# Latent attention: context from unsplit F32 rows in two 64-column halves of the array, row sums added apart, latent queries in column halves

## Chip, core and metric

One Trainium2 chip, one NeuronCore of it. The metric is the device time of one execution in microseconds; lower is better.

## What is computed

Two transformer layers on x (16 batches of 100 rows of 256) with a context of 16 x 1444 rows of 64. Each layer has a cross attention to the context and a mixture of experts. The change touches the attention of the first layer only:

```python
q_hk = (hidden_q @ Wq.T).reshape(Bv, Sv, H, K)            # H = 16 heads
q_big = jnp.einsum('bshk,hkq->bshq', q_hk, w_kc_q)
q_big = _apply_rope(q_big, ...)                           # 192 values a head
kv_r = _apply_rope(kv_c, ...)                             # 1444 keys of 64
q_r = jnp.einsum('bshq,hqr->bhsr', q_big, W_qr)
k_r = jnp.einsum('bld,hdr->bhlr', kv_r, W_kr)
attn = jax.nn.softmax(jnp.einsum('bhsr,bhlr->bhsl', q_r, k_r), axis=-1)
ctx_c = jnp.einsum('bhsl,bld->bhsd', attn, kv_r)
ctx_lat = jnp.einsum('bhsd,hkd->bhsk', ctx_c, w_kc_kv)
return ctx_lat.transpose(0, 2, 1, 3).reshape(Bv, Sv, H * K) @ Wo.T
```

The kernel folds the weights, so that queries and context rows meet in the 64 latent values: a score is a latent query (64) times a rotated context row (64), and the context is softmax weights times the same rotated rows.

## The kernel before

The stages run one behind the other; between them all engines meet. **fold_weights** (L205) makes the folded weights, among them M2, written twice side by side (L237) so that the 64 latent columns fill partitions 0-63 and 64-127.

**latent_queries** (L267) goes over 4 chunks of 400 columns (4 batches x 100 rows) and 16 heads. For each head TensorE makes two halves of 96 rows in split products (twelve F32R matmuls, L175), VectorE multiplies with the rope tables (L353), GpSimd adds (L375), TensorE narrows with M2 in plain F32 (L315), ScalarE rounds to F32R (L385), VectorE subtracts to get the low part in the lower 64 partitions (L344), and SyncE stores the head (L303).

**latent_attention** (L388) goes over 16 batches. A batch's 1600 query columns (16 heads x 100) are cut into 4 groups of 400, the keys into 12 tiles of 128, so a batch has 48 steps. Step n does, in the order in which each engine's program is written:

- TensorE: two score matmuls in F32R (L792 on 128 rows: high query parts and low query parts against the high key part; L793 on 66 rows: the low key part and two rows with the negative row maximum, high and low). For the next batch, one "max piece" (L578), 39 in all, scores without exponential in two banks. Then the values of step n-4: three F32R matmuls (L175 with EH, EL and KVH, KVL) that add high and low parts; the context rows have a column of ones, so that row 64 of the result is the row sum.
- ScalarE: the exponential (L742) to E, and one step later its rounded copy EH (L733).
- GpSimd: EL = E - EH (L501) for 43 of the 48 steps; VectorE does five.
- VectorE: the reduction of each max piece (L599), the rotation of the keys of the batch after next in parts (L527 to L549), the reciprocals of the row sums (L623), the division (L631), the addition to X (L618).

Once a batch the maxima are turned by TensorE (L583), split into MH and ML (L589, L593), and two small DMAs write them into QB (L488). Step 0 of the next batch waits for them. The row sums go by DMA to SR, the reciprocals by DRAM to RS, divided heads to CT, and the projection (L612, 8 F32 matmuls) adds them up. SyncE also loads the queries and the keys (L477) of later batches, in one order written out by hand.

The waits are counted semaphores. Two counts matter here: a max piece waits until the piece two before it is reduced (two banks, FB), and an exponential until the slot in E is free.

## Time and profile before

| | us |
|---|---|
| median of 3 runs | 2293.81 |
| lowest, highest | 2281.6, 2295.21 |
| the profiled execution | 2283.25 |
| its span, first to last instruction | 2281.4 |

| engine | busy us | share of the span |
|---|---|---|
| TensorE, matmuls | 1857.9 | 81% |
| TensorE, weight loads | 1632.6 | 72% |
| VectorE | 1492.1 | 65% |
| ScalarE | 1220.5 | 53% |
| GpSimd | 1117.1 | 49% |

Weight loads run beside matmuls. A matmul's duration has the time that it takes through the array in it, which the next one overlaps, so distances between starts tell what the stream costs. The mean granted TensorE clock is 0.905 of full speed over the span.

### The profile page before, as it was taken

The numbers are of one execution on the slowest core, as the hardware profiler recorded it, in microseconds if no ns is written. First come the engines' busy times: TensorE is split into PE (matmuls) and PEld (weight loads), VectorE is DVE, ScalarE is ACT, GpSimd is POOL, SyncE is SP. The second block draws the span as 40 slices with busy tenths as digits, with TensorE's granted clock in tenths as the row PEclk, the third lists the DMA queues.
The fourth block names the chain that finished last, engine by engine and source line by source line (L and its number), as shares of the span: only waits on it lengthen the run. The fifth ranks groups of instructions, "written<-read, shape, count | busy, mean of one in ns | idle before, by whom it ended". The sixth has DMA issues, their size and how long they took to land. (4 is left out here: it accounts for less than half of the span.)

```text
span 2281.4 us, 38538 instructions
## 1 busy us (share of the span) xinstructions
PE 1857.9 (81%) x10550; PEld 1632.6 (72%) x10550; DVE 1492.1 (65%) x2799; ACT 1220.5 (53%) x2996; POOL 1117.1 (49%) x961
## 2 busy tenths in 40 slices
PE   4999958999999999999999973499993689837870
PEld 3677736888888888888888963499993466626870
DVE  4677777777777777767776433377774466656763
ACT  2111115777777767767777851366661266515650
POOL 0455528888788888878888852300004100014005
PEclk9999967999999999999999985699996599958985
DMA  5522251111111111111110002455542100026654
GB/s 159 197 58 57 55 176 55 63 63 63 45 54 63 64 31 63 63 64 63 63 54 11 16 8 78 140 197 196 204 165 58 34 1 0 0 77 196 198 164 113
DMA packets 115748, 195.76 MB, mean 86 GB/s; under 512 B 48213, under 2 KB 94265, under 8 KB 110161
## 3 DMA queue, kind: packets, MB, share of 16 engines
q1 hardware_dynamic: 107409, 180.88, 24.6%
q0 software_dynamic: 8192, 13.15, 2.0%
q8 instruction: 65, 1.06, 0.2%
q14 instruction: 82, 0.67, 0.1%
HBM read 147.01 MB, written 46.63 MB: 85 GB/s over the span
## 5 line engine op out<-in xcount | busy, mean ns | idle before, releaser
L501 POOL TENSOR_TENSOR EL<-E,EH 128x400 fp32r<-128x400 f32 x688 | 833.4, 1239 | 158.5 <-ACT EH L733 154.0
L599 DVE TENSOR_REDUCE PM<-bank 128x1 f32<-128x482 f32 (+1 forms) x624 | 397.2, 650 | 185.9 <-PE bank L578 182.9
L742 ACT ACTIVATE E<-bank 128x400 f32<-128x400 f32 x768 | 386.4, 503 | 212.8 <-PE bank L793 153.2
L733 ACT ACTIVATE EH<-E 128x400 fp32r<-128x400 f32 x768 | 407.0, 532 | 0.0
L175 PE MATMUL bank<-EH,KVH 128*128 128x400 f32 x768 | 283.1, 369 | 19.8 <-POOL EL L501 18.5
L578 PE MATMUL bank<-KH,QS 128*128 128x482 f32 (+1 forms) x624 | 250.9, 414 | 53.9 <-DVE KVL L549 27.6
L1248 POOL DMA_INDIRECT m_back<-rows_out,m_slots x64 | 64.8, 1013 | 450.8 <-DMA rows_out<-m_ys 421.2
L792 PE MATMUL bank<-QS,KH 128*128 128x400 f32 x768 | 272.1, 354 | 14.9 <-issue 9.1
L793 PE MATMUL bank<-QB,KB 66*128 66x400 f32 x768 | 269.1, 350 | 0.0
L175 PE MATMUL bank<-EH,KVL 128*128 128x400 f32 x768 | 265.7, 346 | 0.0
L175 PE MATMUL bank<-EL,KVH 128*128 128x400 f32 x768 | 265.5, 346 | 0.0
L1232 POOL DMA_INDIRECT rows_in<-m_XN,m_slots x64 | 66.2, 1034 | 340.9 <-POOLq L951 265.6
L375 POOL TENSOR_TENSOR rotated<-rope_prod 96x400 f32<-96x400 f32 x128 | 131.9, 1051 | 169.7 <-DVE rope_prod L353 169.2
L175 PEld LDWEIGHTS bank<-EH,KVH 128*128 128x128 f32 x768 | 146.6, 191 | 64.9 <-POOL EL L501 53.4
L175 PE MATMUL bank<-m_xh,m_UH 128*116 128x256 f32 (+1 forms) x620 | 183.2, 296 | 2.1 <-DVE m_xl L1380 1.4
L175 PE MATMUL bank<-m_xh,m_UL 128*116 128x256 f32 (+1 forms) x620 | 178.0, 287 | 0.0
L175 PE MATMUL bank<-m_xl,m_UH 128*116 128x256 f32 (+1 forms) x620 | 177.8, 287 | 0.0
L578 PEld LDWEIGHTS bank<-KH,QS 128*128 128x128 f32 x624 | 123.6, 198 | 74.5 <-DVE PM L599 43.9
L353 DVE TENSOR_TENSOR rope_prod<-bank,rope_q 96x400 f32<-96x400 f32 x256 | 128.9, 563 | 51.3 <-PE bank L175 51.1
L792 PEld LDWEIGHTS bank<-QS,KH 128*128 128x128 f32 x768 | 146.2, 190 | 20.8 <-issue 10.7
L175 PEld LDWEIGHTS bank<-EL,KVH 128*128 128x128 f32 x768 | 146.2, 190 | 14.5
L793 PEld LDWEIGHTS bank<-QB,KB 66*128 66x128 f32 x768 | 146.2, 190 | 0.6
(244 smaller groups left out, 3983.3 us busy)
## 6 DMA issues: line engine op xcount, KB each, us to landing
m_stage_u<-in_m_up SPq DMA_DIRECT2D x20, 1392.0 KB
raw<-in_ctx_T SPq DMA_DIRECT2D x16, 1444.0 KB, 6.1
m_xg<-rows_in SPq DMA_DIRECT2D x55, 256.0 KB, 4.1
rows_out<-m_ys SPq DMA_DIRECT2D x55, 256.0 KB, 3.7
m_stage_d<-in_m_down SPq DMA_DIRECT2D x20, 696.0 KB
queries<-q_out SPq DMA_DIRECT2D x64, 200.0 KB, 2.4
QS<-queries SPq DMA_DIRECT2D x16, 800.0 KB, 6.1
rows_in<-zeros SPq DMA_DIRECT2D x5, 1792.0 KB
```

The lines of the kernel that those rows point to most:

```text
L175: ins = nc.tensor.matmul(out, lhs, rhs, start=first and n == 0, stop=last and n == len(todo) - 1)
L353: last = nc.vector.tensor_tensor(prod[:, h % 2, n, :].rearrange("p (b s) -> p b s", b=CB), psum[2 * (h % 2) + half][0:HALF, 0:CH].rearrang ...
L375: last = nc.gpsimd.tensor_tensor(rot[:, h % TURNS, half, :], prod[:, h % 2, 2 * half, :], prod[:, h % 2, 2 * half + 1, :], ALU.add)
L501: ops.tensor_tensor(EL[:, n % PB, :], E[:, n % EB, :], as_f32(EH[:, n % PB, :]), ALU.subtract).then_inc(sem, 1)
L578: nc.tensor.matmul(psum[F0 + f % banks][:, 0:KW[j]], QS[r][:, t * P:(t + 1) * P], KH[r][:, sum(KW[:j]):sum(KW[:j + 1])], start=True, stop= ...
L599: nc.vector.tensor_reduce(PM[:, f:f + 1], psum[F0 + f % f_banks(b)][:, 0:KW[f % KC]], AX.X, ALU.max).then_inc(red_done, 1)
L733: nc.scalar.activation(EH[:, n % PB, :], E[:, n % EB, :], ACT.Copy).then_inc(hi_done, 1)
L742: nc.scalar.activation(E[:, n % EB, :], psum[S0 + n % SB][:, 0:CH], ACT.Exp).then_inc(exp_done, 1)
L792: nc.tensor.matmul(out, KH[r][:, keys], QS[r][:, cols], start=True, stop=False)
L793: nc.tensor.matmul(out, KB[r][:, keys], QB[r][:, cols], start=False, stop=True).then_inc(s_ready, 1)
L1232: pool.indirect_dma_start(rows_in[:, :], bass.IndirectOffsetOnAxis(slots[:, n, b:b + 1], 0), XN[:, b, :], None).then_inc(scattered, 16)
L1248: pool.indirect_dma_start(back[:, b % RING, n, :], None, rows_out[0:tiles * TOK, :], bass.IndirectOffsetOnAxis(slots[:, n, b:b + 1], 0)).t ...
```

## The change

**Values.** The exponentials are no longer split into EH and EL, and the context rows no longer into KVH and KVL. One step now covers 800 query columns: of a half batch (p) of 8 heads, the even heads (o = 0) and the odd heads (o = 1), 400 columns each, in two neighbouring banks. One exponential instruction covers both. Two F32 matmuls of 64 output columns each bring the context of the even heads to partitions 0-63 and that of the odd heads to 64-127 of one bank. A batch has 24 steps; TensorE does them in pairs m, with the values of the pair before behind the scores.

**Row sums.** The column of ones is gone. VectorE adds the exponentials of the even heads, four steps at a time (tensor_reduce over a strided view, in two parts of 200 columns), GpSimd those of the odd heads, step by step. A matmul with ones adds up the partitions, for each half batch.

**Order.** Two max pieces a step (EP = 2), still two banks. Ten of twelve parts of the key rotation move from VectorE to GpSimd; the two that make the low key part stay, at steps 18 and 20. The turn of the maxima is in pair 10 of 12, ScalarE's and VectorE's part of it at step 22. The key loads of the batch after go out when the low key part is complete (step 20), the two maxima DMAs behind them.

**Set-up.** KB and QB have 128 rows (maxima in rows 1 and 2, a padding row 0), with more to fill before the first batch; the queries load only after that.

**Latent queries** are narrowed in pairs of heads: the even head to partitions 0-63, the odd one to 64-127, high and low parts in two tiles, four stores a pair. M2 is written once.

```diff
-                    nc.tensor.matmul(psum[2 + h % 2][0:HALF, half * P:(half + 1) * P],
-                                     wqr[:, h, half * HALF:(half + 1) * HALF],
-                                     wkr[:, h, :].rearrange("p (o d) -> p o d", o=1).to_broadcast([R0, 2, DC]),
-                                     start=True, stop=True)
+                    nc.tensor.matmul(psum[2 + h % 2][0:HALF, half * DC:(half + 1) * DC],
+                                     wqr[:, h, half * HALF:(half + 1) * HALF], wkr[:, h, :], start=True, stop=True)
...
+                    for row, part in enumerate((out_h, out_l)):
+                        for o in range(2):
+                            sp.dma_start(queries[bass.ts(c, CB)].rearrange("b p h s -> p h b s")[row * DC:(row + 1) * DC, 2 * j + o],
...
                     for half in range(2):
-                        last = nc.tensor.matmul(psum[4 + h % 2][:, 0:CH], M2[:, half, h, :], rot[:, h % TURNS, half, :],
-                                                start=half == 0, stop=half == 1)
+                        for o in range(2):
+                            h = 2 * j + o
+                            last = nc.tensor.matmul(psum[4 + j % 2][o * DC:(o + 1) * DC, 0:CH], M2[:, half, h, :],
+                                                    rot[:, h % TURNS, half, :], start=half == 0, stop=half == 1)
...
-                        if h >= 2:
-                            narrow(c, h - 2)
+                        if h >= 3 and h % 2:
+                            narrow(c, h // 2 - 1)
...
-    SB, FB = 3, 2
-    EB, PB = 4, 6
-    BEHIND = 4
+    SB, FB = 2, 2
+    GT = 4
+    EB = 2 * GT
+    EP = 2
...
-    TURN_AT, HI_AT = 42, 26
-    RECIP_AT, CT_AT, OUT_AT = 9, 17, 20
-    ROT_AT = (3, 5, 7, 10, 11, 12, 13, 19, 21, 24, 32, 34, 37)
-    LOW_ON_VECTOR = (39, 41, 43, 45, 47)
+    SUM_AT, SUM0_AT, OUT_AT, TURN_AT = 2, 7, 8, 10
+    RECIP_AT, CT_AT = 9, 14
+    ROT_AT = (3, 4, 5, 6, 8, 9, 10, 11, 13, 14)
+    HI_AT, LO_AT = (17, 18), (18, 20)
...
+        def sum_even(v, b, g, part):
+            cols = slice(part * (CH // 2), (part + 1) * (CH // 2))
+            p, q = divmod(g, KT // GT)
...
+                src = R[:, base:base + 1 + GT, 0, cols]
...
+            nc.vector.tensor_reduce(out, src.rearrange("p t c -> p c t"), AX.X, ALU.add).then_inc(even_sum, 1)
+
+        def sum_odd(pool, b, n):
...
+            nc.gpsimd.tensor_tensor(out, first, R[:, slot(n), 1, :], ALU.add).then_inc(odd_sum, 1)
+
+        def sums(pe, b, p):
...
+            for o in range(2):
+                last = nc.tensor.matmul(psum[MISC][o * DC:(o + 1) * DC, 0:CH], ones[:], ES[:, p, o, :], start=True, stop=True)
...
+                def scores(b, n):
...
+                    for lhs, rhs in ((KH, QS), (KB, QB)):
+                        heads = rhs[r][:, p * 2 * CH:(p + 1) * 2 * CH].rearrange("p (j o s) -> p o j s", o=2, s=S)
+                        for o in range(2):
+                            last = nc.tensor.matmul(psum[S0 + 2 * (n % SB) + o][:, 0:CH].rearrange("p (j s) -> p j s", s=S),
+                                                    lhs[r][:, keys], heads[:, o], start=lhs is KH, stop=lhs is KB)
...
-                    split_products(nc, psum[A0 + g % 2][:, 0:CH],
-                                   [(KVH[b_mod(b)][:, cols], KVL[b_mod(b)][:, cols], EH[:, n % PB, :], EL[:, n % PB, :])],
-                                   first=t == 0, last=t == KT - 1).then_inc(av_done, 1)
+                    for o in range(2):
+                        last = nc.tensor.matmul(psum[CTX][o * DC:(o + 1) * DC, 0:CH], KV[b_mod(b)][:, t, :], R[:, slot(n), o, :],
+                                                start=t == 0, stop=t == KT - 1)
+                    last.then_inc(av_done, 1)
...
+                    for m in range(NS // 2):
+                        for n in (2 * m, 2 * m + 1):
+                            scores(b, n)
...
+                            for f in range(EP * n, min(EP * n + EP, NF)):
+                                if has_next:
+                                    max_piece(pe, b + 1, f)
...
+                        for n in (2 * m - 2, 2 * m - 1):
+                            if n >= 0:
+                                values(b, n)
...
                 def step(b, has_next, has_keys):
                     for n in range(NS):
...
+                        pieces = [f for f in range(EP * n, min(EP * n + EP, NF)) if has_next]
+                        for f in pieces:
+                            reduce_piece(v, b + 1, f)
+                        if n % GT < 2:
+                            if n >= GT:
+                                sum_even(v, b, n // GT - 1, n % GT)
```

## Rows read from the trace of the kernel before

**Rows 1.** Windows: PE, PEld, DVE, ACT, POOL busy us (x count), clock, DMA share, GB/s
```profile
100.00:330.00 230.00, 201.32 (x900) 150.62 (x898) 168.33 (x321) 32.00 (x62) 117.42 (x114) 0.95 0.28 82
...
357.00:1375.00 1018.00, 942.80 (x4696) 852.66 (x4696) 705.71 (x959) 750.02 (x1660) 837.30 (x691) 0.98 0.16 51
```

**Rows 2.** Tile ML, window 400:1300: ns min/median/max, first to last start us
```profile
L488 SPq DMA_DIRECT2D QB<-ML x15: 759/804/1093, 417.7 to 1294.9; - x15
```

**Rows 3.** Timeline of attention steps: start us, us, engine, line
```profile
705.14 0.35 PE L792 MATMUL bank<-QS,KH 128*128 128x400 f32 x1
...
705.51 0.38 PE L578 MATMUL bank<-KH,QS 128*128 128x482 f32 x1
...
705.73 0.34 PE L175 MATMUL bank<-EH,KVH 128*128 128x400 f32 x1
...
705.95 0.65 DVE L599 TENSOR_REDUCE PM<-bank 128x1 f32<-128x482 f32 x1
...
711.95 0.34 PE L792 MATMUL bank<-QS,KH 128*128 128x400 f32 x1
```

**Rows 4.** Timeline: the projection's F32 passes, merged
```profile
699.63 3.40 PE L612 MATMUL bank<-BB,CT 128*100 128x256 f32 x15
```

**Rows 5.** Lines by shape, TensorE: busy us, mean ns of one, idle before
```profile
L315 PE MATMUL bank<-rotated,M 96*128 96x400 f32 x256 | 96.2, 500 | 2.2 <-POOL rotated L375 2.2
...
L612 PE MATMUL bank<-BB,CT 128*100 128x256 f32 x256 | 62.4, 400 | 14.0 <-DVE CT L631 14.0
```

**Rows 6.** Waits, window 357:1375: us in total, times, longest us
```profile
PEld bank L175 <- POOL EL L501: 53.4, 136, 1.0
PEld bank L578 <- DVE PM L599: 34.2, 30, 3.8
...
PE bank L792 <- DMA QB<-ML: 5.7, 6, 3.6
```

**Rows 7.** Timeline of the latent queries: one head's narrowing, merged
```profile
90.54 1.51 PE L315 MATMUL bank<-rotated,M 96*128 96x400 f32 x4
```

**Rows 8.** Timeline of the weight folding: one head (in brackets: idle before)
```profile
56.37 0.65 PE L241 MATMUL bank<-wo,wkv 128*64 128x256 f32 x2
56.95 0.46 PEld L237 LDWEIGHTS bank<-wkr,wqr 64*96 64x96 f32 x4 [0.39 <-issue]
...
57.55 0.65 PE L241 MATMUL bank<-wo,wkv 128*64 128x256 f32 x2
```

**Rows 9.** Lines by shape, GpSimd
```profile
L501 POOL TENSOR_TENSOR EL<-E,EH 128x400 fp32r<-128x400 f32 x688 | 833.4, 1239 | 158.5 <-ACT EH L733 154.0
...
L527 POOL TENSOR_TENSOR raw<-raw,ropeT 128x722 f32<-128x722 f32 x4 | 6.7, 1717 | 37.4 <-DMA rawk<-in_ctx_k 37.4
```

**Rows 10.** Lines by shape, VectorE
```profile
L599 DVE TENSOR_REDUCE PM<-bank 128x1 f32<-128x482 f32 x416 | 268.1, 650 | 101.0 <-PE bank L578 99.7
...
L527 DVE TENSOR_TENSOR raw<-raw,ropeT 128x722 f32<-128x722 f32 x60 | 71.4, 1194 | 3.9 <-DMA rawk<-in_ctx_k 3.9
...
L631 DVE TENSOR_TENSOR CT<-CU,RS 64x800 f32<-64x800 f32 x32 | 56.1, 1752 | 11.2 <-DMA RS<-recips 10.9
...
L623 DVE RECIPROCAL RR<-SR 16x100 f32<-16x100 f32 x16 | 12.1, 755 | 7.1 <-DMA SR<-CU 7.1
```

**Rows 11.** Tile raw, window 400:1300: one operation, and the key loads' way to landing
```profile
L538 DVE TENSOR_TENSOR raw<-raw x26: 898/900/902, 447.5 to 1211.0; 128x722 f32<-128x722 f32 x26
...
DMA to landing us min/median/max: 5.8/6.1/6.3
```

**Rows 12.** Timeline of the attention's start: memsets, first maxima, first scores
```profile
310.36 1.26 DVE L824 MEMSET KB<- 2x1444 f32 x1 [0.34 <-issue]
...
320.39 0.34 DVE L829 CAST KVH<-there 128x24 fp32r<-128x24 f32 x3 [1.20 <-DMA there<-in_key_ones]
...
355.13 0.28 DVE L593 TENSOR_TENSOR ML<-bank,MH 13x128 fp32r<-13x128 f32 x1 [0.78 <-ACT MH L589]
...
358.44 0.70 PE L792 MATMUL bank<-QS,KH 128*128 128x400 f32 x1 [3.64 <-DMA QB<-ML]
```

**Rows 13.** Line L303: the latent queries' stores
```profile
L303 SPq DMA_DIRECT2D queries<-q_out x64: 371/372/4186, 83.0 to 304.9; - x64
```

More of the change, by code:

```diff
@@ L52, in __init__ @@
         self.nc, self.ctx = nc, ctx
-        self.psum = [ctx.enter_context(nc.psum_tensor(f"bank{i}", [P, PSUM_COLS], F32)) for i in range(8)]
+        self.banks = ctx.enter_context(nc.psum_tensor("banks", [P, 8, PSUM_COLS], F32))
+        self.psum = [self.banks[:, i, :] for i in range(8)]
         self.stats = fixed(ctx, nc, "stats", [S, B, 6])
@@ L467, in latent_attention @@
         cu_done = core.sem("at_cu")
+        sum_done = core.sem("at_sum")
+        su_done = core.sem("at_su")
         sr_in = core.sem("at_sr")
@@ new lines, in sum_odd @@
+        def sum_odd(pool, b, n):
+            p, t = divmod(n, KT)
+            if t == 0:
+                return
+            pool.wait_ge(exp_done, b_val(b) * NS + (n + 1 + SB))
+            done = b_val(b) * 2 * ADDS + (p * ADDS + t - 1)
+            if t > 1 or p or b is not FIRST:
+                pool.wait_ge(odd_sum, done)
+            if t == KT - 1 and b is not FIRST:
+                pool.wait_ge(sum_done, b_val(b) * 2 + (p - 1))
+            first = R[:, slot(n - 1), 1, :] if t == 1 else EA[:]
+            out = ES[:, p, 1, :] if t == KT - 1 else EA[:]
+            nc.gpsimd.tensor_tensor(out, first, R[:, slot(n), 1, :], ALU.add).then_inc(odd_sum, 1)
@@ L749, in step @@
[L749 to L756 removed]
+                            act.wait_ge(odd_sum, odd_sums_to(before(b), NS + n - EB))
@@ new lines, in step @@
+                        k = S0 + 2 * (n % SB)
+                        nc.scalar.activation(R[:, slot(n), :, :], banks[:, k:k + 2, 0:CH], ACT.Exp).then_inc(exp_done, 1)
+                        if n in HI_AT and has_keys:
+                            keys_high(act, b + 2, HI_AT.index(n))
+                        if n == 1 and b is not FIRST:
+                            context_out(act, before(b), 1)
+                        if n == 2 * SUM_AT + 1 and b is not FIRST:
+                            sums_out(act, before(b), 1)
@@ L808, in step @@
                             turn_max(pe, b + 1)
-                steps(pe, step)
-                for n in range(NS - BEHIND, NS):
-                    values(Batch(0, B - 1), n)
-                project(pe, Batch(0, B - 1))
+                        for n in (2 * m - 2, 2 * m - 1):
+                            if n >= 0:
+                                values(b, n)
+                            elif b is not FIRST:
+                                values(before(b), NS + n)
+                        if m == SUM_AT and b is not FIRST:
+                            sums(pe, before(b), 1)
+                        if m == SUM0_AT:
+                            sums(pe, b, 0)
+                        if m == OUT_AT and b is not FIRST:
+                            pe.wait_ge(su_done, b_val(b) * 2 + 1)
+                            project(pe, before(b))
+                steps(pe, step)
+                for n in range(NS - 2, NS):
+                    values(LAST, n)
+                pe.wait_ge(res_done, B - 1)
+                sums(pe, LAST, 1)
+                pe.wait_ge(su_done, 2 * B)
+                project(pe, LAST)
             @block.vector
```

376 lines of the change are left out of this document (186 added, 190 removed).

## Prediction, made before the changed kernel was run

> **What bounds the kernel now.** I read the engine totals of the page first: TensorE leads. Busy time of matmuls overlaps, so the stages come next: the attention stage takes 1018 us of 2281, TensorE busy 943 of it, and the latent queries before it 230 us [rows 1]. The instruction that loads the low half of the row maxima runs once a batch; its first and last start give (1294.9-417.7)/14 = 62.66 us a batch [rows 2].
>
> What TensorE does in one batch follows from starts, not durations. Six steps with a max piece in each last 711.95-705.14 = 6.81 us, 1.135 a step; the piece of 482 columns takes the stream 0.22 of it, which leaves 0.183 for each of the five F32R matmuls of 400 columns [rows 3]; I count 0.182. The output projection's F32 matmuls count two passes each, the last lasting 0.40, so (3.40-0.40)/14 = 0.215 us a pass [rows 4, 5]. A batch has 48 score steps of 2 matmuls and 48 value steps of 3, so 240 x 0.182 = 43.7 us; 39 max pieces, 8.6; 16 projection passes, 3.4; the turn of the maxima, 0.3. That is 56.0 of 62.66; 6.6 us a batch are waits. The list of waits names them: TensorE waits, most often with the weight load of a matmul, for the low parts EL and for the maxima's reductions, and seldom for the maxima's DMAs [rows 6]. So the stage is bound by TensorE, closely followed by GpSimd (837 us).
>
> **Values.** Before: 144 F32R matmuls a batch, 26.2 us. After: 24 steps of two F32 matmuls of 64 output columns, one into partitions 0-63, one into 64-127. The F32 matmul of 400 columns exists in the latent queries: four passes in 1.51 us, the last lasting 0.50, so (1.51-0.50)/3 = 0.337 us a pass, two passes a matmul [rows 5, 7]. Whether two halves of the array work at once no row shows. One bound: one after the other, 96 x 0.337 = 32.4 us. Other bound: side by side. If matmuls start in order, the two steps of a run (A1 A2 B1 B2 A3 A4 B3 B4, where A and B are the halves) take five slots and not eight, since B1 can go with A2, B2 with A3, B3 with A4, but B4 is alone: 5 x 0.337 = 1.69 us, 12 runs a batch, 20.2 us. I take side by side, because the two write separate partitions and read separate weights, and nothing in the trace makes the second wait. The Trainium skill (TensorE: Matmul & The Clock Gate, Packing small matmuls) says that column tiles start about 4 ns apart and run together; no row here shows it, and its ideal of four slots would make 16.2 us of the 20.2.
>
> **Changes of shape.** In the weight folding, passes on 64 rows alternate with passes that fill 64 columns. From one L241 to the next is 57.55-56.37 = 1.18 us; six passes hold 4x128 + 2x256 columns, 0.86 us at 0.84 ns (0.337/400); between them weight loads stand still for 0.39 us with nothing to wait for [rows 8]. That leaves 0.32 us for two changes, 0.16 each. The context changes to halves and back once per pair of steps: 24 x 0.165 = 4.0 us a batch. The two row-sum pairs follow directly on a context run, three slots each: 2.0 us. The Trainium skill (TensorEngine Tiling (Array Packing), Key Properties) states that changing the tiling mode drains the array; the idle 0.39 us agrees.
>
> TensorE after: scores 96 x 0.182 = 17.5 (same columns; the low product is on 128 rows now and not 66, and L793 with 66 starts at the same pace as the others), values 20.2, changes 4.0, sums 2.0, max pieces 8.6, projection 3.4, turn 0.3: 56.0 us. The old sum again. TensorE gains nothing; what moves are the waits.
>
> **Waits that go.** ScalarE loses 48 rounding copies, VectorE and GpSimd the 48 subtractions that make EL. GpSimd gets 22 additions (1.24 us each) and the rotation's 6,636 columns, at 1717/722 = 2.4 ns: 27 + 16 = 43 us [rows 9], under a batch. The cover: rows of eight steps may wait for it. Its ninth rotation part, for which ScalarE's key copy at step 17 waits, comes at about 10 us (three steps at 2.6, the exponential) + 10 x 1.24 + 5,868 x 0.0024 = 36.5 us; step 17 comes at 44 us. Were that cover gone, exponentials would queue behind the key copy. So the EL waits end.
>
> The context has one bank now, and each half batch's first value matmul waits for its copy on ScalarE; 1.46 us of scores and up to 0.9 of max pieces stand in between, so it costs nothing. The projection's new wait for the row sums' copy has an iteration of cover as well; behind it would stand all scores. SyncE issues two DMAs for one at the divisors and four for two at the queries, 0.4 us each [rows 13], off the path.
>
> **Waits that come: the reductions.** Now four max pieces come in one iteration of two steps, with two banks, and between them VectorE also adds the even rows. Counting from the first piece: a reduction starts 0.44 us after its piece and lasts 0.65 [rows 3, 10]. Pieces at 0 and 0.22; reductions end at 1.09 and 1.74; the third piece, with its load, can start at 1.34 and the fourth at 1.99, where 1.39 to 1.61 was due. From there to the next first piece 0.22 + 0.165 + 1.69 + 0.165 + 0.73 = 2.97. In iterations with a quarter sum, its two parts (800 to 1000 elements, 933 in the mean) stand ahead of reductions. No row has such a strided reduction. Bounds: 1.12 us, as VectorE runs undisturbed (L538's 900 ns for 722 elements less L599's 650 for 482 make 1.04 ns an element, plus 0.15), and 2.0 us, near the 1752/800 ns of the disturbed L631 [rows 10, 11]. I take 1.3, nearer the plain read, since it has one source. Then two iterations last 10.17 us where 8.74 would do: 1.4 lost, five times, 6.8 us a batch (the last iteration has a piece less). At 1.12 it is 6.0, at 2.0 13.8. The reciprocal (0.755 us) sits in the same queue: 0.8 more. The other VectorE work (division, now one instruction of 128x800; two rotation parts) falls where a bank isn't due.
>
> **Waits that come: the maxima's way round.** In the first batch it took 358.44-355.13 = 3.3 us from the low subtraction to the score matmul [rows 12]. Behind the turn TensorE still has 5.5 us of work; ahead of the subtraction VectorE has two sum parts and a rotation part (3.8 us), which just fits. But SyncE issues the next key loads right before, at the twentieth step of 24, and these take 6.1 us to land [rows 11]; if the small DMAs come behind them, the next batch starts about 2.3 us late. Bounds 0 and 3, I take 1.0.
>
> A batch: 56.0 + 6.8 + 0.8 + 1.0 = 64.6 us, +1.95; 16 batches +31 us.
>
> **Latent queries and the ends.** A head costs 12 x 0.182 + 4 x 0.337 = 3.53 us, and the 63 intervals between the first and last query store, (304.9-83.0)/63, make 3.52 us [rows 7, 13]: pure TensorE. After: per pair of heads 8 passes in five slots and two changes, 1.69 + 0.33 against 2.70, so 32 x 0.68 = -22 us. Weight folding computes half the columns of M2: 16 x 4 x 64 x 0.84 ns = -3. Memsets: 1.26 us for 1,444 columns; 8,248 columns a buffer instead of 3,400 make +12.6 us, less the 1.2 us of waiting for a constant that they cover [rows 12] and the KVL part: +10, on the path since queries load only behind them. The last batch's extra matmul and DMAs: +2. Together -13.
>
> 2283.25 (the profiled execution's time, 0.5% under the median of 2293.81) + 31 - 13 = **2301 us**. Measured medians may stand some 10 above. Between 1% under and over the median of before lie 2271 to 2317; that 1% is about what a measurement of this kernel can tell from no change.
>
> **Rivals.**
> *A, the halves overlap fully and changes are free, faster.* Four slots, no 0.165: 56.0 - 4.0 - 14 x 0.337 = 47.3 us. But the reductions' queue stays: after the fourth piece now 2.30 in place of 2.97 us, two iterations last 9.5 us where 7.4 would do, 10.1 us a batch; with the reciprocal's 0.8 and 1.7 for the maxima (less work behind the turn) 59.9 us, -44. Latent queries 32 x 1.35 = -43, ends +9: 2205 us. For it: nothing shows the tail slot. Against it: the standstill in [rows 8]. It decides from about 1.2 us a batch below the forecast on.
> *B, no concurrency, slower.* 32.4 + 2.7 + 29.8 + 4.0 = 68.9, waits 6.5 (the longer runs cover more): 75.4 us, +204; latent queries 32 x 0.33 = +11, ends +9. 2507 us. For it: all F32 rows here are serial. Against it: separate partitions and weights.
> *C, strided sums hold the reductions, slower.* Parts of 2.0 us: 13.8 in place of 6.8, +7 us a batch: 2413 us. At 1.6 us a part it is 10: 2352 us. For it: VectorE's SBUF rows swell beside GpSimd (1194 ns in the mean for 722 columns, [rows 10], against 900). Against it: one source only. The Trainium skill (Vector Engine (DVE) Microarchitecture Reference, Measured stream behaviour on trn2) gives 1.73 ns in place of 1.05 when a source hops every element; an estimate from it is 1.6 us a part. No row here shows such a read.
>
> **Chances.** Forecast (2250 to 2335) 0.45, A 0.22, C 0.18, B 0.15. Of the forecast's 0.45 I put 0.07 under 2271, 0.29 between and 0.09 above 2317. Faster: 0.22 + 0.07 = 0.29. Same: 0.29. Slower: 0.18 + 0.15 + 0.09 = 0.42. The likeliest case's own range is 2250 to 2335; for 8 in 10 the range reaches to A at 2200 and C at 2415 and leaves B out.
>
> **What would show it.** Right: value passes of the two halves whose passes start in pairs 0.34 us apart; a batch of 64 to 65 us; third and fourth pieces waiting for reductions in every iteration; no wait for GpSimd; 3.2 us a head. Wrong: a run of four F32 matmuls over 2.5 us (B), sum parts over 1.6 us (C), context runs of 1.35 us with no gap beside them (A), exponentials waiting for odd sums.

## The result and the profile after

| | before | after |
|---|---|---|
| median, us | 2294.51 (4 runs) | 2380.68 (4 runs) |
| lowest to highest | 2281.6 to 2297.24 | 2379.42 to 2381.73 |
| span of the profiled execution | 2281.4 | 2379.9 |
| mean granted TensorE clock | 0.905 | 0.869 |

After over before is 1.0387, with a 95% interval of 1.0347 to 1.0427: slower by some 86 us. The forecast was 2301, its range 2200 to 2415.

Engine totals of the changed kernel, then its line for the TensorE clock in 40 slices of the span:

```profile
PE 1824.5 (77%) x9910; PEld 1307.4 (55%) x9910; DVE 1531.4 (64%) x2720; ACT 824.3 (35%) x1796; POOL 869.7 (37%) x762
...
PEclk9999859989989989998998997599997599957995
```

ScalarE lost 396 us of work and GpSimd 247, as the change intends, and TensorE's matmuls are busy for 33 us less. None of it shortened the kernel. Before, the attention's slices stood at 0.98 of the full clock [rows 1]; now many stand at 8 and 9 tenths.

The tile of the low maxima, as in [rows 2]:

```profile
L493 SPq DMA_DIRECT2D QB<-ML x16: 752/809/820, 348.7 to 1391.3; - x16
...
  PE banks L816: 79.1, 15
  PEld banks L816: 14.7, 4
```

The last two lines say what waited for this tile: TensorE's matmuls (PE) and its weight loads (PEld), us in total and how often. From first to last start it is (1391.3-348.7)/15 = 69.5 us a batch, where it was 62.6. The attention lost 15 x 6.9 = 104 us. Its first maxima come at 348.7 instead of 356.4, so what lies ahead gained 8. TensorE's matmuls stood 79.1 us for this tile, 5.3 a batch.

The two lines must not be added. A weight load and the matmul behind it can both be listed for one and the same standstill: at 1260.16 us the load has 6.67 us of idle time before it and the matmul 5.97, for the same maxima. In what follows a standstill is the matmul's row; the row of the weight load alone may lie beside a matmul that still runs.

The changed kernel's waits, window 400 to 1400 us (14.4 batches), in total, times, longest:

```profile
PEld banks L562 <- DVE PM L583: 122.3, 199, 2.2
...
ACT CU L646 <- DVE CT L657: 87.8, 14, 6.4
PE banks L816 <- DMA QB<-ML: 75.4, 14, 6.1
...
PE banks L562 <- DVE PM L583: 54.4, 40, 1.9
...
PEld banks L827 <- ACT CU L646: 15.4, 12, 1.3
...
PE banks L827 <- ACT CU L646: 14.0, 14, 1.1
```

The wait for GpSimd's low parts [rows 6] is gone, and three others stand there. A max piece waits for reductions: the matmuls stand 54.4/14.4 = 3.8 us a batch, and the weight loads' 122.3/14.4 = 8.5 lies partly beside running matmuls. The next batch's first score waits for the maxima's DMA. And one value run in each batch waits for the context's copy, 14.0/14 = 1.0 us, because ScalarE waits with it for VectorE's division (the 12 waits of the weight loads are at the same places as 12 of the 14 of the matmuls).

VectorE's sums of the even rows, grouped by shape (L610; a third form, into ES, has 1928 ns):

```profile
L610 DVE TENSOR_REDUCE R<-R 128x200 f32<-128x1000 f32 x64 | 124.9, 1955 | 6.2 <-ACT R L781 5.7
...
L610 DVE TENSOR_REDUCE R<-R 128x200 f32<-128x800 f32 x64 | 101.6, 1589 | 4.8 <-ACT R L781 4.7
```

A part takes 1.59 to 1.96 us, where the forecast had 1.3.

**The values.** A run of eight context passes in the timeline of the changed kernel (start us, us, engine, line):

```profile
705.21 1.56 PE L827 MATMUL banks<-R,KV 128*64 128x400 f32 x8
705.60 0.14 PEld L827 LDWEIGHTS banks<-R,KV 128*64 128x64 f32 x2 [0.19 <-issue]
705.93 0.14 PEld L827 LDWEIGHTS banks<-R,KV 128*64 128x64 f32 x2 [0.19 <-issue]
706.70 0.63 PE L816 MATMUL banks<-QS,KH 128*128 128x400 f32 x2
```

Weights are loaded in pairs, one for each half of the array, 0.33 us apart. From the first pass to the score behind the run 706.70-705.21 = 1.49 us go by: four slots of 0.337 and one change of shape of 0.14 to 0.16. So the halves run side by side, and there is no fifth slot. The Trainium skill (TensorE: Matmul & The Clock Gate, Packing small matmuls) has column tiles run together; the trace agrees, with 1.49 us for eight passes that take 2.70 one after the other.

**The end of a batch.** The turn of the maxima and the next batch's start, same kernel and columns:

```profile
471.08 1.95 DVE L610 TENSOR_REDUCE R<-R 128x200 f32<-128x1000 f32 x1
...
473.06 0.91 DVE L541 TENSOR_TENSOR KB<-raw,KH 64x722 fp32r<-64x722 f32 x1
...
474.00 2.00 DVE L610 TENSOR_REDUCE R<-R 128x200 f32<-128x1000 f32 x1
...
474.15 0.34 SPq L482 DMA_DIRECT2D raw<-in_ctx_T  x1
...
474.68 0.33 SPq L483 DMA_DIRECT2D rawk<-in_ctx_k  x1
...
475.89 0.27 DVE L577 TENSOR_TENSOR ML<-banks,MH 13x128 fp32r<-13x128 f32 x1
476.18 0.88 SPq L493 DMA_DIRECT2D QB<-MH  x1
...
477.12 0.81 SPq L493 DMA_DIRECT2D QB<-ML  x1
...
482.07 1.03 PE L816 MATMUL banks<-QS,KH 128*128 128x400 f32 x2 [5.78 <-DMA QB<-ML]
```

The key loads go out at 474.15 and 474.68, while the subtraction still stands behind VectorE's last sum part; the two small DMAs stand behind them, and the score waits until 482.07, 4.95 us from the issue of the second. In the first batch before, with nothing ahead, it took 3.3 us from the low subtraction to the score [rows 12]; here 482.07-475.89 = 6.2.

**The clock.** Stretches of the same kernel, columns as in [rows 1] (the clock is the third number from the end):

```profile
482.00:488.00 6.00, 5.93 (x18) 4.42 (x20) 3.80 (x5) 1.68 (x2) 0.98 (x1) 0.51 0.00 0
511.00:515.00 4.00, 3.35 (x10) 1.30 (x10) 2.41 (x5) 0.00 (x0) 4.00 (x3) 0.59 0.21 47
525.00:529.00 4.00, 3.56 (x12) 1.24 (x12) 0.92 (x2) 1.84 (x3) 2.73 (x2) 0.57 0.01 4
700.00:705.00 5.00, 4.11 (x20) 2.42 (x16) 4.99 (x7) 2.40 (x4) 2.52 (x3) 1.00 0.00 0
...
500.00:1200.00 700.00, 588.48 (x2522) 348.72 (x2520) 479.67 (x573) 228.44 (x307) 384.86 (x316) 0.91 0.16 51
```

Three times in the batch that begins at 482.07 the granted clock falls to the lower level (1.2 of 2.4 GHz): with the standstill of 5.78 us for the maxima, after 1.83 us for a reduction at 511.65, and after 1.18 and 1.00 us for a reduction and the context's copy at 523.38 and 525.44. There a run of eight context passes lasts 2.94 us instead of 1.56. Over 700 us the mean is 0.91. With two levels, 1 and 0.5, this is 18% of the time at the lower one, 12.5 us of a batch. It costs up to half of that, 6.3 us; what of it falls into a standstill costs nothing more. Before, the same stretch had 0.99.

**What the batch loses, term by term.** The starts of the matmuls in the trace allow a finer count. Each distance from one matmul's start to the next is set against the distance that the same pair of instructions keeps at full clock when nothing waits (the shortest tenth). The excess belongs to the wait that ended there, or, where the lower level was granted and nothing waited, to the clock. For the changed kernel, over 15 batches, this gives 7.6 us a batch for reductions (the 3.8 above is only the part in which no matmul is recorded; a matmul's duration covers a short standstill behind it), 4.8 for the maxima, 1.1 for the context's copy and 4.8 for the clock. What is left of 69.5 is 51.3 us of work at full clock; the same count on the kernel before leaves 56.

### The profile page after: what moved, and what is told of

The parts are those of the page before. It is cut to its first block and busy times, and to the rows that moved or that the text cites. A ratio compares the mean times of both kernels' runs of the same rounds, so it can differ in the third digit from the quotient of the medians.

```text
span 2379.9 us, 34375 instructions
## 1 busy us (share of the span) xinstructions
PE 1824.5 (77%) x9910; PEld 1307.4 (55%) x9910; DVE 1531.4 (64%) x2720; ACT 824.3 (35%) x1796; POOL 869.7 (37%) x762
## 5 line engine op out<-in xcount | busy, mean ns | idle before, releaser
L583 DVE TENSOR_REDUCE PM<-banks 128x1 f32<-128x482 f32 (+1 forms) x624 | 379.3, 651 | 317.3 <-PE banks L562 316.5
L781 ACT ACTIVATE R<-banks 128x800 f32<-128x800 f32 x384 | 315.6, 839 | 545.5 <-PE banks L816 527.6
L625 POOL TENSOR_TENSOR EA<-EA,R 128x400 f32<-128x400 f32 x288 | 312.3, 1084 | 299.9 <-ACT R L781 293.1
L562 PE MATMUL banks<-KH,QS 128*128 128x482 f32 (+1 forms) x624 | 255.8, 465 | 111.7 <-DVE PM L583 58.3
L827 PE MATMUL banks<-R,KV 128*64 128x400 f32 x1536 | 326.5, 549 | 14.9 <-ACT CU L646 14.9
L816 PE MATMUL banks<-QS,KH 128*128 128x400 f32 x768 | 238.9, 394 | 79.2 <-DMA QB<-ML 79.1
L610 DVE TENSOR_REDUCE R<-R 128x200 f32<-128x1000 f32 (+1 forms) x128 | 226.4, 1772 | 10.9 <-ACT R L781 10.5
L816 PE MATMUL banks<-QB,KB 128*128 128x400 f32 x768 | 211.4, 358 | 0.0
L176 PE MATMUL banks<-m_xh,m_UH 128*116 128x256 f32 (+1 forms) x620 | 184.1, 297 | 11.4 <-issue 10.0
L176 PE MATMUL banks<-m_xh,m_UL 128*116 128x256 f32 (+1 forms) x620 | 178.6, 288 | 0.0
L610 DVE TENSOR_REDUCE ES<-R 128x200 f32<-128x1000 f32 x64 | 123.1, 1928 | 6.6 <-ACT R L781 6.6
```

The lines of the kernel that those rows point to most:

```text
L176: ins = nc.tensor.matmul(out, lhs, rhs, start=first and n == 0, stop=last and n == len(todo) - 1)
L562: nc.tensor.matmul(psum[F0 + f % n][:, 0:KW[j]], QS[r][:, t * P:(t + 1) * P], KH[r][:, sum(KW[:j]):sum(KW[:j + 1])], start=True, stop=True ...
L583: nc.vector.tensor_reduce(PM[:, f:f + 1], psum[F0 + f % f_banks(b)][:, 0:KW[f % KC]], AX.X, ALU.max).then_inc(red_done, 1)
L610: nc.vector.tensor_reduce(out, src.rearrange("p t c -> p c t"), AX.X, ALU.add).then_inc(even_sum, 1)
L625: nc.gpsimd.tensor_tensor(out, first, R[:, slot(n), 1, :], ALU.add).then_inc(odd_sum, 1)
L781: nc.scalar.activation(R[:, slot(n), :, :], banks[:, k:k + 2, 0:CH], ACT.Exp).then_inc(exp_done, 1)
```

## The experiments

Period is the time of one batch of the attention (first to last start of the maxima's low DMA, over 15). The clock is the mean granted over 500 to 1200 us of the profile. Ratios are against the kernel before on the same chip.

| | median us | ratio (95%) | period us | clock |
|---|---|---|---|---|
| before | 2278 to 2295 | 1 | 62.6 | 0.99 |
| after | 2380.68 | 1.0387 (1.0347 to 1.0427) | 69.5 | 0.91 |
| 1 latent queries alone | 2253.77 | 0.9886 (0.9837 to 0.9936) | 62.6 | 0.99 |
| 2 sums in memory order | 2256.23 | 0.9898 (0.9864 to 0.9932) | 62.8 | 0.95 |
| 3 maxima first | 2330.32 | 1.0233 (1.019 to 1.0277) | 67.3 | 0.92 |
| 4 one half of the array | 2449.03 | 1.0745 (1.07 to 1.079) | 74.0 | 1.00 |
| 5 low part early | 2356.9 | 1.0326 (1.0282 to 1.037) | 69.2 | 0.92 |
| 6 pieces apart | 2350.42 | 1.0247 (1.0216 to 1.0277) | 67.4 | 0.91 |
| 7 sums as additions | 2336.31 | 1.0175 (1.0142 to 1.0208) | 67.0 | 0.93 |
| 8 = 3 + 5 | 2298.14 | 1.002 (1.0001 to 1.004) | 64.2 | 0.96 |
| 9 = 3 + 5 + 7, division early | 2273.67 | 0.9916 (0.9893 to 0.994) | 62.6 | 0.96 |
| 10 = 3 + 5 + 2 | 2182.75 | 0.9567 (0.9523 to 0.961) | 57.5 | 1.00 |
| 11 = 3 + 5, division early | 2254.7 | 0.9885 (0.9837 to 0.9934) | 62.1 | 0.99 |
| 12 = 11 + 6 | 2182.55 | 0.9556 (0.9511 to 0.9601) | 57.6 | 1.00 |

The loss of each, counted as above from the starts of the matmuls, in us a batch (an estimate; each term may be off by some tenths):

| | reductions | maxima | copy | clock | left of the period |
|---|---|---|---|---|---|
| after | 7.6 | 4.8 | 1.1 | 4.8 | 51.3 |
| 2 sums in memory order | 3.3 | 4.5 | 1.1 | 2.5 | 51.4 |
| 3 maxima first | 7.5 | 2.7 | 1.1 | 4.7 | 51.5 |
| 4 one half of the array | 3.9 | 1.4 | 1.1 | 0.3 | 67.3 |
| 5 low part early | 7.2 | 4.8 | 1.1 | 4.7 | 51.4 |
| 6 pieces apart | 4.0 | 5.6 | 2.9 | 4.6 | 50.4 |
| 7 sums as additions | 6.5 | 4.6 | 0.9 | 3.8 | 51.3 |
| 8 = 3 + 5 | 8.2 | 1.1 | 1.0 | 2.4 | 51.6 |
| 9 = 3 + 5 + 7, division early | 7.7 | 1.0 | 0 | 2.5 | 51.5 |
| 10 = 3 + 5 + 2 | 3.6 | 1.0 | 1.1 | 0.3 | 51.6 |
| 11 = 3 + 5, division early | 8.5 | 1.2 | 0 | 0.7 | 51.8 |
| 12 = 11 + 6 | 3.9 | 1.9 | 0 | 0.2 | 51.6 |

The theory in them: two waits, for the reductions behind the strided sums and for the maxima's DMAs behind the key loads, make up the loss. The rivals: TensorE's own amount has grown (fifth slots, no concurrency), or GpSimd has become the bound.

**1, the latent queries alone.** The kernel before with fold_weights and latent_queries of the changed one (M2 of 64 columns a head, narrowing in pairs into two halves, four stores a pair).

> The kernel before with only the latent queries (and M2) in column halves; the attention is the old one. Theory (halves run pass beside pass in four slots, two changes of shape at 0.16 us a pair): a pair of heads 6.03 us instead of 7.05, 32 pairs, -33 us, so about 2261 against 2294. Rival (the four stores a pair in place of two, or the later low part, hold the queue): no gain or less than 10 us. Rival (five slots, as predicted): -22 us.

The first maxima's DMA started at 335.6 us instead of 356.4, and the period stayed at (1274.2-335.6)/15 = 62.6. So this part gains 21 us up to there, ratio 0.9886, and the loss of 104 us is the attention's. The number alone would have spoken for the rival with five slots (-22); the distances decide for four. The timeline of the changed kernel has the price of a change of shape: from the last of one head's F32R matmuls to the second behind the narrowing,

```profile
86.96 0.34 PE L176 MATMUL banks<-XH_a,AL 128*96 x1
...
87.23 1.56 PE L321 MATMUL banks<-rotated,M 96*64 96x400 f32 x8
...
88.99 0.34 PE L176 MATMUL banks<-XL_a,AH 128*96 x1
```

88.99-86.96 = 2.03 = 2 x 0.18 + 4 x 0.337 + 0.32: four slots and two changes of 0.16. Per pair it saves 2.70 - 1.35 - 0.32 = 1.03 us, 33 in all; with the folding's 3 that would be 36. At the borders of the four chunks the narrowing now waits 8.2 us in all for GpSimd, and the clock falls there, which it did not before. The stage before and in experiment 1, columns as in [rows 1]:

```profile
83.00:305.00 222.00, 218.32 (x976) 163.55 (x974) 159.19 (x307) 31.78 (x63) 126.08 (x123) 1.00 0.28 83
```

```profile
83.00:284.00 201.00, 189.11 (x965) 131.75 (x963) 134.33 (x272) 15.63 (x31) 124.13 (x121) 0.95 0.36 87
```

A clock of 0.95 over 201 us costs up to 10 us. Waits and clock together, up to 18, cover the 15 that are missing.

**2, the sums in memory order.** The same elements are read, but in the order in which they lie, so each output adds neighbours:

```diff
-            nc.vector.tensor_reduce(out, src.rearrange("p t c -> p c t"), AX.X, ALU.add).then_inc(even_sum, 1)
+            k = GT if q == 0 else GT + 1
+            nc.vector.tensor_reduce(out.rearrange("p (t c) -> p t c", t=k), src.rearrange("p t (c k) -> p t c k", k=k),
+                                    AX.X, ALU.add).then_inc(even_sum, 1)
```

> The changed kernel, with the even heads' sums read in the order of memory: the same elements, the same number of outputs, but each output adds neighbours (so the row sums are not the true ones). Theory (the stride makes a part 1.59 to 1.95 us, and this holds the reductions): a part falls to about 1.1 us, the reductions' waits fall by about 7 us a batch and the maxima's subtraction comes earlier, together 8 to 9 us a batch, 2380 to about 2245. Rival (the stride costs nothing, the number of elements does): parts stay above 1.5 us and the time within 10 us of 2380. Rival (batches are held by the maxima's way alone): parts fall, the time by less than 50 us.

```profile
L611 DVE TENSOR_REDUCE R<-R 128x200 f32<-128x1000 f32 x64 | 75.8, 1189 | 7.4 <-ACT R L783 7.0
...
L611 DVE TENSOR_REDUCE R<-R 128x200 f32<-128x800 f32 x64 | 62.4, 977 | 7.1 <-ACT R L783 7.1
```

The stride alone made the difference: for each element (1955-1589)/200 = 1.8 ns against (1189-977)/200 = 1.06. GpSimd, which works beside it, does not matter to the strided read: of the changed kernel's reductions of 128x1000, 5 have no GpSimd instruction beside them and take 1.83 to 1.97 us, and 17 have one throughout and take 1.92 to 1.98. The loss to reductions fell from 7.6 to 3.3 us a batch and that to the clock from 4.8 to 2.5; the maxima hardly moved (4.8 to 4.5), which I had expected to come earlier too. The period fell by 6.8 us where 8 to 9 were expected, the median by about 5%. The Trainium skill (Vector Engine (DVE) Microarchitecture Reference, Measured stream behaviour on trn2) has, for an operation of two sources, 1.73 ns where one of them hops every element and 1.05 where none does; the runs, with one source, agree within 0.1.

**3, the maxima first.** SyncE issues the maxima's two DMAs ahead of the key loads.

```diff
                     if has_keys:
-                        sp.wait_ge(k_ready, b_val(b) + 3)
-                        ...
-                            key_loads(sp, b_val(b + 3))
-                    if has_next:
-                        max_rows(sp, b_val(b + 1), b_mod(b + 1))
+                    if has_next:
+                        max_rows(sp, b_val(b + 1), b_mod(b + 1))
+                    if has_keys:
+                        sp.wait_ge(k_ready, b_val(b) + 3)
+                        ...
+                            key_loads(sp, b_val(b + 3))
```

> The changed kernel, with the two maxima DMAs ahead of the next key loads in SyncE's program. Theory (the small DMAs stand behind 1.8 MB of keys): the wait at a batch's start falls from 6 to about 3 us (what VectorE's late subtraction leaves), and the clock is cut less: -45 to -75 us, so 2305 to 2335. Rival (VectorE's queue alone makes them late): no change, 2375 to 2385. Rival (the key loads, now later, hold the next rotation): slower than 2381.

Its timeline at the same place as above:

```profile
473.89 0.27 DVE L577 TENSOR_TENSOR ML<-banks,MH 13x128 fp32r<-13x128 f32 x1
474.18 0.89 SPq L493 DMA_DIRECT2D QB<-MH  x1
...
475.12 0.81 SPq L493 DMA_DIRECT2D QB<-ML  x1
476.20 0.34 SPq L482 DMA_DIRECT2D raw<-in_ctx_T  x1
...
477.24 0.64 PE L817 MATMUL banks<-QS,KH 128*128 128x400 f32 x2 [2.97 <-DMA QB<-ML]
```

From the subtraction to the score 477.24-473.89 = 3.35 us, as in [rows 12]; behind the key loads it was 6.2. The loss to the maxima fell from 4.8 to 2.7 us a batch; the rest of it is a subtraction that comes late behind a sum part of 2 us. Period -2.2 us. By its ratio the run gained 35 us, less than the 45 to 75 expected, since the clock rose only from 0.91 to 0.92.

**5, the low part early.** VectorE subtracts at step 21, ahead of a sum part, and the DMAs stay behind the key loads.

```diff
+                        if n == 2 * TURN_AT + 1 and has_next:
+                            max_low(v, b + 1)
                         if n % GT < 2:
...
-                        if n == 2 * TURN_AT + 2 and has_next:
-                            max_low(v, b + 1)
```

> The changed kernel, with only VectorE's low subtraction ahead of the sum part of step 21; the key loads stay ahead of the maxima's DMAs. Theory (the small DMAs land with the key loads, whatever VectorE does, as long as they are issued behind them): the key loads go out at the same time as before, so the wait at a batch's start falls by less than 0.7 us a batch, 2365 to 2381. Rival (the two delays simply add): -2.0 us a batch and less of the clock's cut, 2330 to 2345.

The loss to the maxima stayed at 4.8 us a batch and the period came to 69.2, 0.3 less. With the key loads ahead, the place in VectorE's queue is worth next to nothing.

**8, both (3 and 5).**

> The changed kernel with two changes of order: the maxima's DMAs ahead of the key loads (as in the run before), and VectorE's low subtraction ahead of the sum part of step 21. Theory (the two queues add up: 2.9 us by the key loads, 2.0 by VectorE's sum part): the wait at a batch's start falls from 6 over 3.4 to about 1.4 us, 2380 - 50 - 30 = 2300. Rival (behind the subtraction something else is late, the turn itself or ScalarE): as with the DMAs alone, 2325 to 2345.

The loss to the maxima fell from 4.8 to 1.1 us a batch and that to the clock from 4.8 to 2.4, while reductions took 0.6 more; the period fell to 64.2, 5.3 us less. The edits are worth 2.2 and 0.3 one by one and 5.3 together: two queues in a row, of which the slower one hides the other.

**4, one half of the array.** Both value matmuls go into partitions 0 to 63, and the odd heads' own context is left out.

```diff
-                        last = nc.tensor.matmul(psum[CTX][o * DC:(o + 1) * DC, 0:CH], KV[b_mod(b)][:, t, :], R[:, slot(n), o, :],
-                                                start=t == 0, stop=t == KT - 1)
+                        last = nc.tensor.matmul(psum[CTX][0:DC, 0:CH], KV[b_mod(b)][:, t, :], R[:, slot(n), o, :],
+                                                start=t == 0 and o == 0, stop=t == KT - 1 and o == 1)
```

> The changed kernel, with both value matmuls of a step into partitions 0 to 63 (the even and odd heads' contexts are added up there, which leaves the odd heads' own context out). Theory (two halves run at once): eight passes take eight slots again, 2.7 us a run instead of 1.35, 12 runs, 16 us a batch, less what the longer run covers of other waits: 2380 to 2550 to 2640. Rival (the halves never overlap): within 10 us of 2381.

```profile
706.59 2.90 PE L827 MATMUL banks<-R,KV 128*64 128x400 f32 x8
...
706.98 0.14 PEld L827 LDWEIGHTS banks<-R,KV 128*64 128x64 f32 x1 [0.20 <-issue]
```

Now the loads come singly (the next of this kind at 707.32, 0.34 us later), and the eight passes take 2.90 us instead of 1.56: serial passes. That is rival B's machine, and it shows by contrast that the changed kernel's halves are concurrent. It adds 12 x 1.34 = 16.1 us of TensorE to a batch, but the period grew by 4.5 only, far less than expected: the reductions took 3.9 us in place of 7.6, the maxima 1.4 in place of 4.8, and the clock 0.3 in place of 4.8, at a granted 1.00. An engine that loses 18 us a batch to waits and the clock can be given 16 us of work for 4.5.

**6, the pieces apart.** The second step's two max pieces go behind the value run, so that no four come in a row.

```diff
-                            for f in range(EP * n, min(EP * n + EP, NF)):
-                                if has_next:
-                                    max_piece(pe, b + 1, f)
+                            if n % 2 == 0:
+                                for f in range(EP * n, min(EP * n + EP, NF)):
+                                    if has_next:
+                                        max_piece(pe, b + 1, f)
...
+                        for f in range(EP * (2 * m + 1), min(EP * (2 * m + 1) + EP, NF)):
+                            if has_next:
+                                max_piece(pe, b + 1, f)
```

> The changed kernel, with the third and fourth max piece of an iteration behind the value matmuls and not ahead of them; VectorE's program stays. Theory (four pieces within 1.6 us meet two banks, so TensorE stands until reductions are done): the waits for reductions, 12.6 us a batch in the changed kernel, fall by a third or more, 3 to 5 us a batch, 2380 to 2300 to 2330. Rival (VectorE simply has 8 x 0.65 + 2 x 1.85 = 8.9 us of work in two iterations, where TensorE has 8.0, and the order doesn't matter): less than 1 us a batch, 2365 to 2385.

The period fell by 2.1 us. Its waits, window 400 to 1400:

```profile
PE banks L816 <- DMA QB<-ML: 87.8, 15, 6.8
...
PEld banks L562 <- DVE PM L583: 81.0, 194, 1.1
...
PE banks L827 <- ACT CU L646: 46.2, 15, 3.3
PEld banks L827 <- ACT CU L646: 42.6, 12, 3.6
```

The reductions took 4.0 us a batch in place of 7.6. But the context's copy took 2.9 in place of 1.1 and the maxima 5.6 in place of 4.8: -3.6 + 1.8 + 0.8 = -1.0, and -0.2 for the clock; the remaining 0.9 lies in the column that is left. More than half of the gain was given back at the next waits in line, the division ahead of the copy above all.

**7, the sums as additions.** The four-step sum becomes additions of contiguous blocks of 128x800 (two steps each), a last one folds the two halves: no stride, and the sums remain complete.

```diff
-                src = R[:, base:base + 1 + GT, 0, cols]
...
+            pair = [R[:, base + 2 * k:base + 2 * k + 2, 0, :] for k in range(2)]
...
+                    nc.vector.tensor_tensor(AC[:], AC[:], pair[0], ALU.add).then_inc(even_sum, 1)
...
+                nc.vector.tensor_tensor(AC[:], AC[:], pair[1], ALU.add).then_inc(folded if last else even_sum, 1)
```

> The changed kernel, with the even heads' sums made by contiguous additions of 128x800 (two a quarter, one more of 400 at the end) in place of the strided reductions; the result is the true one. Theory (the stride is the cost, not the number of elements): a 128x800 addition takes 1.0 to 1.2 us where a part took 1.59 to 1.95, 5 to 6 us of VectorE instead of 11 for a half batch; the gain is that of the run that read in the order of memory, -100 to -130 us, 2250 to 2280. Rival (two-source reads beside GpSimd's additions swell to 1.7 us and more, on both engines): 2330 or slower.

```profile
L630 POOL TENSOR_TENSOR EA<-EA,R 128x400 f32<-128x400 f32 x288 | 346.7, 1204 | 265.5 <-ACT R L786 257.5
...
L610 DVE TENSOR_TENSOR AC<-AC,R 128x800 f32<-128x800 f32 x64 | 109.7, 1714 | 0.6
...
L606 DVE TENSOR_TENSOR AC<-AC,R 128x800 f32<-128x800 f32 x64 | 79.4, 1240 | 16.5 <-ACT R L786 16.5
```

Period -2.5 us, a third of what experiment 2 gave. One shape has means from 1240 to 1714 ns, and GpSimd's additions of 128x400 went from 1.08 to 1.20 in the mean. The timeline of the same run shows when an addition is slow:

```profile
618.82 0.98 DVE L606 TENSOR_TENSOR AC<-AC,R 128x800 f32<-128x800 f32 x1
620.17 1.03 POOL L630 TENSOR_TENSOR EA<-R 128x400 f32<-128x400 f32 x1 [9.59 <-ACT R L786]
...
647.00 1.75 POOL L535 TENSOR_TENSOR raw<-raw 128x722 f32<-128x722 f32 x1
647.52 2.08 DVE L606 TENSOR_TENSOR AC<-AC,R 128x800 f32<-128x800 f32 x1
```

Of the 160 additions of 128x800, 16 have no GpSimd instruction beside them: all take 0.98 us. Of the 44 that have one throughout, 39 take over 1.6. So the two engines hold each other up when VectorE adds from two sources in SBUF. No run took GpSimd's part away, but the contrast within this one leaves little else.

**9, order, additions and an earlier division** (`RECIP_AT, CT_AT = 7, 12` in place of 9, 14).

> The changed kernel with all: maxima's DMAs first, low subtraction first, contiguous additions, reciprocals at step 7 and division at step 12 in place of 9 and 14. Theory (three separate causes that add up: sums 6.8 us a batch, the maxima's way 6, its cut of the clock and the context's copy some 2): 69.5 - 14 = 55 to 58 us a batch, 2165 to 2215 us, which is under the kernel before. Rival (they hide one another; the reductions' bank wait takes what the others give): 2230 to 2260, equal to the additions alone.

The expectation had 55 to 58 us a batch, its rival 2230 to 2260 us, and the result is slower than both. The period is 62.6 us, that of the kernel before, and the gain of the median (0.8%) is about that of the latent queries: with the order right and no stride, but with the slow additions, the new attention is worth the old one.

**10, order and sums in memory order (2, 3 and 5).**

> The changed kernel with both changes of order and the even heads' sums read in the order of memory (row sums not the true ones). Theory (strided sums and the maxima's way are separate causes): their gains add, -6.8 and -5.2 us a batch, 69.5 to 57.5, about 2380 - 111 - 82 = 2187. Rival (both end in the same wait, the earlier reductions only move it to the maxima): 2215 to 2250.

Experiment 2 took about 111 us from the changed kernel, 8 about 84, each by its ratio; together 195, and here it is 188 (0.0820 of 2290). The two causes add up, and without them the change is 4.3% faster than before instead of 3.9% slower.

**11, order and the earlier division, strided sums kept.**

> The changed kernel with both changes of order, reciprocals at step 7 and division at step 12 in place of 9 and 14; sums strided. Theory (the context has one bank, and its copy waits for the division, TensorE 2 us a batch for the copy): -1 to -2 us a batch against the run with the order alone (2298), 2265 to 2285. Rival (the division only takes the place of another VectorE job in the same queue): 2290 to 2300.

Against 8 the period fell by 2.1 us. The value run's wait for the copy, 1.0 us a batch in 8, is gone, and the clock takes 0.7 in place of 2.4.

**12, order, earlier division, pieces apart.** It computes what the changed kernel computes and keeps the strided sums.

> A version meant to be fast, with the true result: the changed kernel with both changes of order, the third and fourth max piece behind the values, reciprocals at step 7 and division at step 12. Theory (each takes its own wait): order 82, pieces 30, division some 15 to 25 us: 2380 to 2245 to 2255, level with the old attention behind the new latent queries (2254 beside a before of 2278). Rival (VectorE's strided sums bound the first twenty steps at 8.9 us in two iterations, nothing more is to be had): 2270 to 2300.

Waits of 12, window 400 to 1400, of which the attention fills 870 us, 15.1 batches, and its clock over 500 to 1200:

```profile
PEld banks L562 <- DVE PM L583: 106.9, 237, 1.1
...
PE banks L817 <- DMA QB<-ML: 27.2, 14, 2.5
```

```profile
500.00:1200.00 700.00, 659.28 (x3085) 393.55 (x3084) 598.60 (x699) 279.30 (x373) 457.88 (x376) 1.00 0.18 57
```

The median is 2182.55 us, 4.4% under the kernel before (3.9 to 4.9) and 8% under the changed one. I had expected 2245 to 2255. The pieces apart are worth 4.5 us a batch here, against 2.1 in experiment 6: the reductions fall from 8.5 (experiment 11) to 3.9, and with the division ahead no wait for the copy takes it back. The clock is 1.00 in place of 0.91. Of the 11.9 us between the periods of after and 12, the reductions account for 3.7, the maxima for 2.9, the copy for 1.1 and the clock for 4.6, 12.3 together.

## Why the prediction came out as it did

**Right.** The kind of the outcome: TensorE gains nothing that reaches the end, the waits decide. The sign only just: 2301 is 0.3% over the median before, and slower had the largest chance, 0.42; measured are 3.9%. The time lies inside the range for 8 in 10, but outside the 2250 to 2335 of the likeliest case. The range holds it because rival C was priced into it, and, as shown below, C's numbers fit for the wrong sum. The halves run side by side (1.49 against 2.90 us, experiment 4). A change of shape costs 0.16 us, read from the weight folding's standstill [rows 8]. The wait for GpSimd disappears and GpSimd is not the bound. The third and fourth max piece wait for reductions. The memsets' cost: the max pieces of the first batch start 8 us earlier than before, where the latent queries alone gained 21, so about 13 went into set-up; the forecast had 10.

**The run's fifth slot: wrong.** I let matmuls start in order and left B4 alone. The passes of both halves start together from the first pair on, and a run takes four slots: 12 x 0.337 = 4.0 us a batch less, and two row-sum pairs with two slots each instead of three, another 0.7 (in the trace a pair runs from 497.69 to the score at 498.46, 0.77 us with the change of shape). TensorE's stream is then 56.0 - 4.7 = 51.3 us. The experiments agree: less waits and clock, all periods but those of 4 and 6 leave 51.3 to 51.8. The latent queries gained 33 by the same count where 22 were forecast, and gave back up to 18 at the chunk borders to GpSimd and the clock, which I had not looked for.

**The sum part: mis-sized, and the wait right by luck.** 1.3 us was taken, 1.59 to 1.96 measured, 1.82 in the mean of all three forms. That is rival C, priced at 2352 to 2413, and I had set it aside because VectorE's slow rows [rows 10] had two sources. The reason held for that cause (experiment 7) and left out the other, the stride. By the forecast's own bounds (10 us at 1.6, 13.8 at 2.0) parts of 1.82 would make 12.1 us of waits for reductions, with the reciprocal 12.9. Measured are 7.6, just what was forecast: too short a part and too dear a price for it cancelled. Experiment 2 shows the price alone: parts of 1.12 us lose 3.3, where the sum had 6.0 + 0.8 for them. So 2381 lies among C's numbers, but the stride was worth 4.3 us of waits and 2.3 of clock a batch, and the rest came from elsewhere.

**The maxima's way: mis-sized most of all.** 1.0 us was taken within bounds of 0 and 3, and 4.8 measured (5.3 by the matmuls' idle time). The parts were on the table: the key loads ahead on the queue [rows 11], 3.8 us of VectorE work, 5.5 us of TensorE work behind the turn. The bound was wrong, since I reckoned with about 2.3 us behind the key loads and with sum parts of 1.3. With parts of 2.0 the subtraction comes at 475.89, 4.5 us after the turn, the DMAs land 5 us after the issue of the second, and TensorE, whose runs are shorter by a slot each, is done sooner. All of it pushes one way.

**The clock: missing.** The forecast priced each wait by its length. A standstill of 5.8 us, and in places one of 1.8, is followed by work at the lower level. This is 4.8 us a batch, as much as the maxima's wait itself.

**The context's bank: wrong at small size.** "Costs nothing" became 1.1 us a batch: the copy stands behind the division in ScalarE's queue, and the division behind reductions and sum parts in VectorE's. It follows from the sum part, and experiment 11 removes it.

**The sum, again.** Forecast 56.0 + 6.8 + 0.8 + 1.0 = 64.6. Measured 69.5 = 51.3 + 7.6 + 4.8 + 1.1 + 4.8, but for rounding. Against the forecast the stream is 4.7 us shorter, the reductions with the reciprocal are as forecast, and the maxima (+3.8), the copy (+1.1) and the clock (+4.8) are 9.7 more. What is left, 4.9 x 16 = 78 us, is nearly all of the 80 by which the forecast missed.

## What to carry to other kernels

Where an edit relieves the engine that bounds the kernel, price the queues of the engines that feed it next, with the duration of the new instruction taken at its own access pattern: a strided read of SBUF was priced as a plain one here. Small transfers on which the critical engine waits go ahead of large ones in the queue, and an early place in one queue is worth nothing while the next is late. Edits that each look small can be large together (2.1 us alone and 4.5 behind another), so after each gain look in the list of waits for who took it back before dropping it. And don't add the waits of weight loads to those of matmuls: both can be one standstill, and the sum then explains more than the time that was lost.

## What the runs showed of the hardware

- Eight F32 passes of 400 columns in two 64-column halves: 1.35 us and 0.16 for the change of shape; into one half only 1.34 more.
- tensor_reduce on VectorE over F32 in SBUF: 1.06 ns an element in memory order, 1.8 ns with the reduced axis strided by 800 elements, with or without GpSimd work beside it.
- tensor_tensor on VectorE, F32 128x800 from two sources in SBUF (experiment 7): 0.98 us with GpSimd idle, mostly over 1.6 us and up to 2.4 with GpSimd at work beside it.
- TensorE's clock: after a standstill of 5.78 us a granted 0.51 over the next 6 us, and the same lower level after waits of 1.83 us and of 1.18 with 1.00. In experiment 12, with waits of up to 1.1 us for reductions and 2.5 for the maxima, the mean over 700 us is 1.00.
- A wait can be cheaper filled than left: 16 us more matmuls a batch cost 4.5 (experiment 4).
